# A tower layer on one core: new hand-written engine sequences, with the inner quantisation on GpSimd, the input rounding on ScalarE, and the down result split over ScalarE and GpSimd

## What is computed

```python
# dynamic convolution block: softmax over 31 taps for 16 heads, taps run over the images
a = h @ w1.T + b1
w = softmax(a @ ww.T + bw)            # 16 heads x 31 taps
y = sum_k w[..., k] * shifted(a, k)
y = y @ w2.T + b2
attn = layer_norm(h + y) * gamma + beta
h = layernorm(h + attn)               # "mid" norm
# feed-forward block, weights rounded to -1, 0, 1, activations to 8 bits
q1 = round(h * 127 / max|h|)          # per row
g = silu(q1 @ wg) * (q1 @ wu)         # 1024 inner columns, rescaled
q2 = round(g * 127 / max|g|)          # per row
out = layernorm(h + (q2 @ wd) * scale)
```

## Time and profile before

| | us |
|---|---|
| median of 3 runs | 152.15 (152.15 to 153.42) |
| the profiled execution, its own time | 152.89 |
| its span, first to last instruction | 151.0 |
| mean granted TensorE clock | 0.955 of full |
| busy TensorE, VectorE, ScalarE, GpSimd | 121.8, 98.0, 74.3, 53.7 |

### The profile page before, as it was taken

One profiled execution on the slowest core, in us unless ns is written; L12 is line 12 of the kernel. 1 busy time (PEld: TensorE's weight loads), 2 busy tenths in 40 slices (PEclk: granted clock), 3 DMA queues, 4 the chain that ended last, 5 costly groups with the idle time before them and its releaser, 6 DMA issues. The chain is left out here.

```text
span 151.0 us, 2274 instructions
## 1 busy us (share of the span) xinstructions
PE 121.8 (81%) x722; PEld 73.6 (49%) x730; DVE 98.0 (65%) x256; ACT 74.3 (49%) x113; POOL 53.7 (36%) x102
## 2 busy tenths in 40 slices
PE   7799999899989899898599599757966886667930
PEld 2385547655857736645363374345443362313520
DVE  5057769937407248849839655785688787897641
ACT  0311864682611139439827952883364454736410
POOL 7950002416614301701704440661651454404130
PEclk9999999999999999999999969978999999978995
DMA  4999992255323300121121113012210100100011
GB/s 133 397 333 434 419 412 92 47 57 209 35 51 57 32 4 0 35 26 15 35 25 10 35 45 29 7 36 50 20 32 0 39 0 0 35 0 17 25 35 35
DMA packets 22314, 12.44 MB, mean 82 GB/s; under 512 B 18013, under 2 KB 20317, under 8 KB 21918
## 3 DMA queue, kind: packets, MB, share of 16 engines
q1 hardware_dynamic: 21504, 10.72, 25.2%
q10 hardware_dynamic: 798, 1.58, 3.2%
HBM read 9.95 MB, written 2.34 MB: 81 GB/s over the span
## 5 line engine op out<-in xcount | busy, mean ns | idle before, releaser
L974 POOL TENSOR_SCALAR veps<-mv 128x1 f32<-128x1 f32 x24 | 5.8, 242 | 59.9 <-DVE mv L726 33.1
L610 ACT ACTIVATE silu<-bank,sc 128x512 f32<-128x512 f32 x16 | 11.0, 688 | 18.5 <-PE bank L417 18.5
L417 PE MATMUL bank<-w_q,q1T 128*128 128x512 bf16 x57 | 16.5, 412 | 3.2 <-ACT q1T L602 2.9
L439 PE MATMUL bank<-ident,gu 128*128 128x128 f32 x64 | 10.8, 298 | 7.6 <-ACT gu L574 7.5
L686 DVE TENSOR_REDUCE top<-bank 128x16 f32<-128x496 f32 x8 | 5.3, 667 | 17.5 <-PE bank L352 17.5
L298 PE MATMUL bank<-xT,tokW 128*128 128x256 f32 x72 | 16.3, 380 | 0.0
L366 PE MATMUL bank<-conv_w,vpad 128*32 128x128 f32 x256 | 15.7, 397 | 0.0
L298 PEld LDWEIGHTS bank<-xT,tokW 128*128 128x128 f32 x72 | 13.6, 190 | 2.6 <-issue 0.9
L352 PE MATMUL bank<-wl,h1T 128*128 128x496 f32 x32 | 14.6, 579 | 0.0
L581 ACT ACTIVATE q2T<-bank,minus_magic 128x512 bf16<-128x512 f32 x15 | 10.3, 689 | 7.5 <-PE bank L439 7.2
L975 POOL TENSOR_TENSOR rstd<-veps,minus_half 128x1 f32<-128x1 f32 x24 | 13.2, 549 | 2.0
(11 more groups left out here) (108 smaller groups left out, 231.2 us busy)
## 6 DMA issues: line engine op xcount, KB each, us to landing
xT<-in_xT SPq DMA_DIRECT2D x3, 768.0 KB, 14.7
w_raw<-in_wg SPq DMA_DIRECT2D x1, 1024.0 KB, 11.4
w_raw<-in_wu SPq DMA_DIRECT2D x1, 1024.0 KB, 13.4
w_raw<-in_wd SPq DMA_DIRECT2D x1, 1024.0 KB, 16.7
shear<-taps SPq DMA_DIRECT2D x8, 128.0 KB, 1.8
conv_w<-shear SPq DMA_DIRECT2D x64, 16.0 KB, 1.9
out_dram<-res SPq DMA_DIRECT2D x8, 128.0 KB
xT<-in_xT ACTq DMA_DIRECT2D x2, 384.0 KB, 5.6
```

The source lines that it names most:

```text
L417: last = nc.tensor.matmul(out, q1T[:, t % 2, k, :], w_q[:, j, at:at + HALF], start=(k == 0), stop=(k == KC - 1))
L439: last = nc.tensor.transpose(ps_q2T(t, half)[:, k * P:(k + 1) * P], gu[:, t % 2, half, k * P:(k + 1) * P], ident[:])
L610: nc.scalar.activation(silu[:, t % 2, half, :], ps_gate, ACT.Silu, scale=sc[:, t % 2, 2:3]).then_inc(silu_ok, 1)
```

## The change

The loops are gone. Each engine gets one list of calls written out, in an order of its own. The embeds are spread through the first 60 calls, the tap work (`logits`, `exps`, `normalise`) is done for all tiles by the time the feed-forward of tile 2 starts, and the feed-forward of tile `t` runs beside the attention of tiles `t+2` and later. Gate and up of each half, and both halves of down, are now single calls that can lie apart.

Work that moves to another engine:

- `quant_inner` for tiles 0 to 6: ScalarE to GpSimd (14 operations of 128x512). Tile 7 stays on VectorE (half 0) and ScalarE (half 1).
- the last step of `quant_in`: VectorE to ScalarE (8 operations of 128x256).
- `down_result` for tiles 0 to 6: instead of one VectorE operation, ScalarE reads PSUM times scale into `f` (`scaled_down`) and GpSimd adds `h3` (`add_h3`).

Work that goes: eight of the final keep-warm matmuls, the memset of `no_taps` (zeros now come from `conv_w`), and four of the ten table loads. The values no longer share a bank with the attention accumulator but with the logits (bank 2); `down` has bank 0 from its start. `q2T`, `stats`, `mv`, `veps`, `rstd` have two buffers, `sc` four. The DMA of the second pair of images is issued ahead of the feed-forward weights, and that of the fourth pair ahead of the first taps.

```diff
-        ps_down = bank[0][:, D:2 * D]
-        ps_v = bank[1][:, 0:D]
-        ps_attn = bank[1][:, D:2 * D]
+        ps_down = bank[0][:, 0:D]
+        ps_attn = bank[1][:, 0:D]
+        ps_v = bank[2][:, 0:D]
...
+            sp.dma_start(xT[:, 1], xT_d[1]).then_inc(x_in[1], 16)
             sp.dma_start(w_raw[:, 0], wg_d).then_inc(ffn_in[0], 16)
             sp.dma_start(w_raw[:, 1], wu_d).then_inc(ffn_in[1], 16)
-            sp.dma_start(xT[:, 1], xT_d[1]).then_inc(x_in[1], 16)
...
+            embed(0, 0); embed(0, 1); logit_bias(); logit_weights(); values(0); residual(0); logits(0)
+            embed(1, 0); weight_means(0, 2); logits(1); embed(1, 1); values(1); embed(2, 0); logits(2); conv(0)
+            logits(3); project_out(0); weight_means(2, 3); embed(2, 1); residual(1); conv(1); logits(4)
+            project_out(1); embed(3, 0); in_transposes(0); values(2); gate(0, 0); up(0, 0); values(3)
+            residual(2); up(0, 1); gate(0, 1); conv(2); logits(5); in_transposes(1); project_out(2); gate(1, 0)
+            up(1, 0); values(4); residual(3); embed(3, 1); up(1, 1); gate(1, 1); conv(3); logits(6)
+            project_out(3); inner_transposes(0, 0); in_transposes(2); logits(7); inner_transposes(0, 1); conv(4)
+            residual(4); down(0, 0); down(0, 1); project_out(4); gate(2, 0); up(2, 0); in_transposes(3)
...
+            conv(7); down(2, 0); down(2, 1); project_out(7); gate(5, 0); up(5, 0); inner_transposes(3, 0)
+            up(5, 1); gate(5, 1); in_transposes(6); inner_transposes(3, 1); gate(6, 0); up(6, 0); down(3, 0)
+            down(3, 1); inner_transposes(4, 0); up(6, 1); gate(6, 1); inner_transposes(4, 1); in_transposes(7)
+            down(4, 0); down(4, 1); inner_transposes(5, 0); gate(7, 0); up(7, 0); inner_transposes(5, 1)
+            up(7, 1); gate(7, 1); down(5, 0); down(5, 1); inner_transposes(6, 0); inner_transposes(6, 1)
+            down(6, 0); down(6, 1); inner_transposes(7, 0); inner_transposes(7, 1); down(7, 0); down(7, 1)
...
+            def quant_in(t):
+                act.wait_ge(q1_scale_ok, t + 1)
...
+                nc.scalar.activation(q1[:], centred[:, t % 2, :], ACT.Identity, bias=magic[:, 0:1],
+                                     scale=sc[:, t % 4, 7:8]).then_inc(q1_ok, 1)
...
+            def scaled_down(t):
+                act.wait_ge(down_ps, t + 1)
+                act.wait_ge(down_scale_ok, t + 1)
...
+                nc.scalar.activation(f[:, t % 3, :], ps_down, ACT.Identity,
+                                     scale=sc[:, t % 4, 9:10]).then_inc(down_read, 1)
...
+            def quant_inner(t, half):
+                pool.wait_ge(q2_scale_ok, t + 1)
+                nc.gpsimd.tensor_scalar(gu[:, t % 2, half, :], gu[:, t % 2, half, :], sc[:, t % 4, 8:9], MAGIC,
+                                        ALU.mult, ALU.add).then_inc(q2_ok, 1)
+            def add_h3(t):
+                pool.wait_ge(down_read, t + 1)
+                pool.wait_ge(h3_ok, t + 1)
+                nc.gpsimd.tensor_tensor(f[:, t % 3, :], f[:, t % 3, :], h3[:, t % 3, :], ALU.add).then_inc(f_ok, 1)
...
+            inv_std_attn(7); scale_h3(5); inv_std_out(2); quant_inner(4, 0); result(1); inv_std_mid(7)
+            result(2); quant_inner(4, 1); add_h3(3); quant_inner(5, 0); quant_inner(5, 1); inv_std_out(3)
+            add_h3(4); scale_h3(6); result(3); quant_inner(6, 0); quant_inner(6, 1); inv_std_out(4); result(4)
+            scale_h3(7); add_h3(5); add_h3(6); inv_std_out(5); result(5); inv_std_out(6); result(6)
+            inv_std_out(7)
```

More of the change, by code:

```diff
@@ L291, in _ @@
         def _(pe):
+            put = dict(values=0, logits=0, conv=0, q1T=0, gate=0, down=0, embed0=0, embed4=0)
             def embed(pair, m):
-                pe.wait_ge(x_in[pair], 16)
-                if pair > 0 or m > 0:
-                    pe.wait_ge(h1T_ok, 2 * pair + m if pair == PAIRS - 1 else max(2 * pair + m - 1, 1))
+                i = 2 * pair + m
+                if pair > 0:
+                    pe.wait_ge(x_in[pair], 16)
+                if m == 0 or pair == PAIRS - 1:
+                    if put["embed0"]:
+                        pe.wait_ge(h1T_ok, put["embed0"])
+                    if put["down"]:
+                        pe.wait_ge(down_read, put["down"])
+                    put["embed0"] = i + 1
+                else:
+                    if put["embed4"]:
+                        pe.wait_ge(h1T_ok, put["embed4"])
+                    if put["gate"]:
+                        pe.wait_ge(silu_ok, put["gate"])
+                    put["embed4"] = i + 1
                 for k in range(KC_PATCH):
+                    if i == 0 and k in (0, 3):
+                        pe.wait_ge(tokW_in[k // 3], 16)
+                        pe.wait_ge((x0_in, x_in[0])[k // 3], 16)
                     last = nc.tensor.matmul(ps_embed(pair, m), tokW[:, k, m * P:(m + 1) * P], xT[:, pair, k, :],
@@ L340, in values @@
                 last.then_inc(v_ps, 1)
+                put["values"] += 1
             def logits(t):
@@ L353, in logits @@
                 last.then_inc(logits_ps, 1)
+                put["logits"] += 1
             def conv(t):
@@ L398, in in_transposes, with gate @@
                 last.then_inc(q1T_ps, 1)
-            def gate_up(t):
+                put["q1T"] += 1
+            def gate(t, half):
+                if t == 0 and half == 0:
+                    pe.wait_ge(wq_gate_ok, 1)
+                pe.wait_ge(h1T_ok, put["embed4"])
+                pe.wait_ge(q1T_ok, t + 1)
+                if t > 0 or half > 0:
+                    pe.wait_ge(silu_ok, 2 * t + half)
+                for k in range(KC):
+                    at = k * INNER + half * HALF
+                    last = nc.tensor.matmul(ps_gate, q1T[:, t % 2, k, :], w_q[:, 0, at:at + HALF],
+                                            start=(k == 0), stop=(k == KC - 1))
+                last.then_inc(gate_ps, 1)
+                put["gate"] += 1
@@ L459, in down @@
                                             start=(k == 0), stop=(k == KC_INNER - 1))
-                last.then_inc(down_ps, 1)
-            def keep_warm(out, count):
-                for _ in range(count):
-                    nc.tensor.matmul(out, ones_bf[:], ones_bf[:, 0:1].broadcast_to([P, 512]), start=True, stop=True)
+                if half == 1:
+                    last.then_inc(down_ps, 1)
+                    put["down"] += 1
             pe.wait_ge(ones_ok, 1)
-            keep_warm(bank[7][:, :], WARM_UP)
@@ new lines, in _ @@
+            in_transposes(4); inner_transposes(1, 0); values(6); inner_transposes(1, 1); up(3, 1); gate(3, 1)
+            down(1, 0); down(1, 1); conv(6); residual(6); gate(4, 0); up(4, 0); project_out(6); in_transposes(5)
+            inner_transposes(2, 0); up(4, 1); gate(4, 1); values(7); inner_transposes(2, 1); residual(7)
+            conv(7); down(2, 0); down(2, 1); project_out(7); gate(5, 0); up(5, 0); inner_transposes(3, 0)
+            up(5, 1); gate(5, 1); in_transposes(6); inner_transposes(3, 1); gate(6, 0); up(6, 0); down(3, 0)
@@ new lines, in _ @@
+            nc.gpsimd.memset(conv_w[:], 0.0).then_inc(pool_zeros_ok, 1)
+            normalise(0); normalise(1); add_beta(0); inv_std_attn(0); inv_std_mid(0); normalise(2)
+            weight_finish(0, wclip_gate, wq_gate_ok); add_beta(1); inv_std_attn(1); weight_round(2)
+            inv_std_mid(1); normalise(3); normalise(4); add_beta(2); inv_std_attn(2); scale_h3(0)
+            quant_inner(0, 0); scale_h3(1); add_beta(3); inv_std_mid(2); scale_h3(2); quant_inner(0, 1)
+            weight_finish(2, wclip_down, wq_down_ok); normalise(5); inv_std_attn(3); inv_std_mid(3); add_beta(4)
@@ new lines, in _ @@
+            add_h3(0); inv_std_attn(4); normalise(6); inv_std_mid(4); normalise(7); quant_inner(1, 0)
+            add_beta(5); quant_inner(1, 1); scale_h3(3); inv_std_out(0); inv_std_attn(5); quant_inner(2, 0)
+            inv_std_mid(5); add_h3(1); result(0); add_beta(6); scale_h3(4); quant_inner(2, 1); inv_std_attn(6)
+            quant_inner(3, 0); quant_inner(3, 1); inv_std_out(1); inv_std_mid(6); add_beta(7); add_h3(2)
+            inv_std_attn(7); scale_h3(5); inv_std_out(2); quant_inner(4, 0); result(1); inv_std_mid(7)
```

807 lines of the change are left out of this document (360 added, 447 removed).

## The result

The changed kernel takes **127.73 us** (127.36 to 127.84), against 152.78 for the kernel before in the same set of runs: a ratio of 0.836, interval 0.830 to 0.841. The forecast was 131.0, with 125 to 141 as its range. The profiled execution took 127.84 us, its span is 125.4, its mean granted clock 0.989. They leave out the slow executions, except in one set (the two other moves undone, and the first two changes of the end), whose ratios of 0.828 to 0.834 therefore read 0.005 to 0.01 too low.

A forecast was written before the change was run, and what follows sets the result against it. The prediction took the second half as bound by engine-to-engine hand-overs. Walk 126.7 plus clock 2.2 plus GpSimd-VectorE hindrance 1.5 gave span 130.4; plus 1.9, less 0.7, then rounding given back: 131.0 us, range 125 to 141.

The forecast's parts named there:

- The mechanism: Second half of the layer: no engine full, engine-to-engine hand-overs inside one step bind; the new order is the large term.
- The walk: All engines' new lists played against each other with profiled durations, giving start times and a span of 126.7 us.
- gave back a tenth: VectorE steps were rounded up by 5 us in all; a tenth was taken off, giving 131.0.
- The clock: TensorE at 2.4 GHz to about 107 us, then a lower stretch in the last 13 us: 2.2 us added.
- GpSimd and VectorE in each other's way: Exposed VectorE centring and norm, two a tile, slowed while GpSimd works: 2.8 us, half where VectorE is late, 1.5.
- Prices of the moved operations: Inner rounding on GpSimd 0.75 us, its h3 addition 0.73; on ScalarE input rounding 0.50, down scaling 0.47.
- The steps from span to median: From span 130.4: plus 1.9 for the profiled execution, less 0.7 to the median, 131.6; then rounding given back, 131.0.
- A: The forecast itself: TensorE and VectorE near full, hand-overs hidden; 131.0 us, 125 to 135; chance 0.66.
- C: Tiles 2 to 7 keep TensorE's present waits because list durations do not hold: 12 more, 143 us; chance 0.09.
- D: TensorE's shorter waits from 40 to 120 us hold it at 1.2 GHz: 155 us or more; chance 0.04.
- B: GpSimd's strict queue becomes the bound from tile 3 on; 140.5 us if locks cost their full bound; chance 0.19.
- the 6 that the prediction had set: Sign of being wrong: TensorE or VectorE naming GpSimd in their waits for over 6 us.

The follow-up runs named there:

- the two other moves undone: The changed kernel with one move back on VectorE each time: input rounding, 128.53 us (0.834), or down result as one operation, 127.84 us (0.830).
- the first two changes of the end: The changed kernel with quant_inner(4, 1) ahead of result(1) and result(2) on GpSimd, 127.99 us; then also result(6) moved to VectorE, 127.61 us.
- the split alone: The kernel before, old loops kept, with the new owners of inner rounding, input rounding and down result: 152.14 us, ratio 0.993.
- the first variant of the end: The changed kernel with quant_inner(4, 1) put ahead of result(1) and result(2) in GpSimd's list: 127.99 us, ratio 0.832.

## Why the prediction was right

**The mechanism held, and its place too.** The prediction said that the layer in its second half was bound by hand-overs, and that the gain is the order. The order with the buffers and banks that go with it gives 128.09 us, the split alone 152.14, and taking the fillers out of three tiles costs 4.3. TensorE is busy 32.9 of 33.5 us where it had 26.3.

**The walk.** Its stations were close all along: conv(0) 33.1 against 33.45 measured, logits(7) 69.3 against 69.61, conv(7) 95.3 against 94.33, the wait of inner_transposes(4,1) 1.4 against 2.02, the last result's end 123.6 against 122.4. Span 126.7 against 125.4. The difference arises in one stage: logits(7) came 0.3 us later than in the walk and gate(6,0), 101.66 for 103.3, 1.6 sooner. TensorE is idle for only 0.6 us from 70 to 103.5, so the short waits that the walk put there hardly came. The longer wait for `quant_inner(4, 1)` then took 0.6 back. The prediction knew that its VectorE steps were rounded up by 5 us in all and gave back a tenth; that they made those waits fits, and no run here shows it.

**The clock, 2.2 us: mis-sized in this execution.** The granted clock is 1.00 from 103.5 to 122.5, in spite of waits of 2.02 and 1.34 us. The variant with the input rounding on VectorE shows the forecast case: the same wait, then pieces at the lower level, and 1.5 us lost. The mis-sized step is "I expect a lower stretch in the last 13 us": what the rows carried was that it can fall there, not that it does. That it stayed up in the profiled execution is luck as far as these runs tell.

**GpSimd and VectorE in each other's way, 1.5 us: real in VectorE's rows, little of it on the path.** In the changed kernel's tile view of `h1b` and `centred` (lowest, median and highest ns) and in its timeline:

```profile
L734 DVE SCALAR_TENSOR_TENSOR a<-a,rstd,h1b x8: 476/484/1505, 40.5 to 100.7; 128x256 f32<-128x256 f32 x8
...
L753 DVE TENSOR_SCALAR centred<-a,mv x8: 347/368/797, 41.7 to 102.9; 128x256 f32<-128x256 f32 x8
```

```profile
47.94 1.97 POOL L1043 TENSOR_SCALAR w_raw<-w_raw,w_scale 128x2048 f32<-128x2048 f32 x1
...
48.68 1.50 DVE L734 SCALAR_TENSOR_TENSOR a<-a,rstd,h1b 128x256 f32<-128x256 f32 x1
...
115.63 0.94 DVE L829 TENSOR_SCALAR gu<-gu,sc 128x512 f32<-128x512 f32 x1
```

The norm of two SBUF inputs takes 0.48 us alone and 1.50 beside a GpSimd operation that ends at 49.9, not long before the norm does. By the means, 0.66 and 0.48, eight norms lost 1.4 us and eight centrings 0.9 to 1.0; with the 0.46 that the last rounding lost, some 2.8 us, which is what the prediction had as a whole (16 x 0.5 x 0.35). But it said that half of it lands on the path. TensorE is 99% busy from 37.8 to 103.5, where 16 of the 17 lie, so little of it does. The chain that ended last holds the norm at 48.68 and a centring of 0.64 at 52.78, together 1.3 us over their length alone, but it goes on to TensorE at 59.4, which had stood for only 0.17 us there. The last rounding is not in it, although TensorE waits for it. How much of the 1.5 reached the time was not measured; these rows leave room for little. The Trainium skill, SBUF — State Buffer, "Who interferes with whom", describes this as a lock on a shared pair of ports that lasts for an instruction; this trace agrees in kind, with 1.50 against 0.48.

GpSimd loses by it too, and the prediction had no term for that. From before to after, the mean of `normalise` goes from 0.64 to 0.85 us, of `add_beta` from 0.73 to 0.85 and of the inverse root from 0.55 to 0.60, about 4 us over 8, 8 and 24 of them. Nearly all of it lies in four operations that ran beside VectorE's work on a weight (28 to 31 and 51 to 53 us). And when the last rounding on VectorE starts first, as in the first variant of the end (114.76 against 114.79), it keeps its 0.48, and GpSimd's `result` takes 0.80 where the changed kernel shows 0.55.

**Prices of the moved operations.** Groups of the changed kernel (count, busy us, mean ns of one):

```profile
L1031 POOL TENSOR_SCALAR gu<-gu,sc 128x512 f32<-128x512 f32 x14 | 10.1, 725 | 0.4
...
L1038 POOL TENSOR_TENSOR f<-f,h 128x256 f32<-128x256 f32 x7 | 5.3, 756 | 1.8 <-ACT f L640 1.8
L601 ACT ACTIVATE q<-centred,magic,sc 128x256 f32<-128x256 f32 x8 | 4.8, 600 | 2.6 <-DVE sc L772 2.4
...
L640 ACT ACTIVATE f<-bank,sc 128x256 f32<-128x256 f32 x7 | 3.3, 472 | 1.4 <-PE bank L512 1.2
```

Inner rounding 0.725 against 0.75, addition 0.76 against 0.73, down scaling 0.47 as taken. The input rounding is 0.60 where 0.50 was taken. The nearest row was `q1T`, which reads PSUM and takes one value per partition, a bias; this one reads SBUF and takes two, scale and bias. In the changed kernel a plain copy of 256 columns out of PSUM takes 0.37 us and `q1T` 0.47, so one such value seems to cost 0.10; the exponential of 496 columns out of SBUF takes 0.62 and a copy of 496 out of PSUM 0.57, both without one, so the source seems to cost half of that. No run separates the two. It lay inside the bounds of 0.40 to 0.81 and was covered. Engine totals: VectorE 92.7 against "near 90", ScalarE 65.2 against 65, GpSimd 71.3 against 69.

**The sum.** 126.7 + 2.2 + 1.5 = 130.4 of span was forecast, 125.4 measured: 1.3 too much in the walk, 2.2 for a clock that did not fall, 1.5 for a hindrance that by the rows was nearly all covered. All three point the same way, 5.0 us in all. The steps from span to median gave 1.7 back: 0.6 was added for them (1.9 less 0.7 and 0.6; a tenth of 5 is 0.5, rounded to 131.0) and 2.3 is what the median lies above the span. So 5.0 less 1.7 is the 3.3 between 131.0 and 127.7, inside A's own range of 125 to 135.

**The rivals.** C, hand-overs stay, fell: TensorE's longest wait from 16.8 to 103 us is under 0.7. D, the clock, fell: 1.00 in all stages. B, GpSimd as the bound, fell by its size, 140.5 us, and by little else. TensorE and VectorE wait 5.9 us for it in all (2.2 for `gu`; 1.6, 1.5 and 0.2 for `rstd`; 0.4 for `f`), just under the 6 that the prediction had set, and that without the 1.0 that TensorE waits for `ones_bf` at the start of either kernel. The chain that ended last runs through GpSimd from 81 us on, and 0.75 us more a rounding brings 8.9 us, 1.5 of them by the clock. Moving its roundings to ScalarE gives nothing.
